# Attention with the values as the loaded operand and the output scaled by reciprocals spread from memory

## The reference

```python
q = (xn @ Wq).reshape(b, n, HEADS, DIM_HEAD).transpose(0, 2, 1, 3)
k, v = (kv[..., :DIM_HEAD], kv[..., DIM_HEAD:])
q = l2norm(q) * q_scale
k = l2norm(k) * k_scale
sim = jnp.einsum('bhid,bjd->bhij', q, k) * SCALE + attn_bias     # causal and masked
attn = jax.nn.softmax(sim, axis=-1)
out = jnp.einsum('bhij,bjd->bhid', attn, v)
return ln(out.reshape(b, n, HEADS * DIM_HEAD) @ Wout, g_out)
```

## Time and profile before

| what | value |
|---|---|
| median of 3 runs | 2564.28 us |
| profiled execution, first to last instruction (span) | 2563.2 us |
| attention, from the first scores to the first delta projection | 55 to 1101 us |
| TensorE busy, share of the span | 93% |
| VectorE / ScalarE / GpSimd busy | 68% / 48% / 52% |

### The profile page before, as it was taken

The page is one execution under the profiler, slowest core; times in us unless marked ns, Lnnn a source line. Parts: engine busy times, 40 slices in busy tenths (PEclk is TensorE's granted clock), DMA queues, the critical chain, the costliest instruction groups (busy, mean ns, idle before and its releaser), DMA issues. The chain is left out here.

```text
span 2563.2 us, 56453 instructions
## 1 busy us (share of the span) xinstructions
PE 2394.0 (93%) x20705; PEld 1977.5 (77%) x20705; DVE 1753.9 (68%) x4121; ACT 1234.0 (48%) x3133; POOL 1333.1 (52%) x1464
## 2 busy tenths in 40 slices
PE   5999999999999999977999999988899999999998
PEld 3788888888888888845777777766677877778776
DVE  4576767677767676677888888337865755746764
ACT  3656666666666666554555555114333333332332
POOL 3676767676767676535666666215422322322332
PEclk8999999999999999988999999999999999999999
DMA  4000100000000000001122221216022112111211
GB/s 143 7 11 9 46 18 11 10 10 9 11 10 9 10 5 5 5 15 24 40 56 55 55 53 47 55 59 181 32 66 63 55 58 67 58 47 62 66 34 59
DMA packets 156689, 105.05 MB, mean 41 GB/s; under 512 B 85168, under 2 KB 134832, under 8 KB 156416
## 3 DMA queue, kind: packets, MB, share of 16 engines
q1 hardware_dynamic: 130928, 62.69, 9.0%
q10 hardware_dynamic: 25488, 38.73, 4.9%
HBM read 80.51 MB, written 20.88 MB: 40 GB/s over the span
## 5 line engine op out<-in xcount | busy, mean ns | idle before, releaser
L968 POOL TENSOR_TENSOR a_bm<-a_bias,a_mask_add 128x512 f32<-128x512 f32 (+3 forms) x512 | 438.4, 873 | 189.3 <-DVE a_nm L697 186.3
L1592 POOL TENSOR_TENSOR m_hid_part<-m_hid,m_hid_part 128x512 fp32r<-128x512 f32 x176 | 238.5, 1355 | 552.9 <-ACT m_hid_part L1501 547.6
L874 ACT ACTIVATE a_S<-a_S,a_nm 128x512 f32<-128x512 f32 (+3 forms) x512 | 289.3, 565 | 347.6 <-DVE a_nm L697 344.9
L697 DVE CUSTOM_DVE_ANT_0 a_S<-a_S,a_bm,a_nsn 128x512 f32<-128x512 f32 (+3 forms) x512 | 275.3, 545 | 142.1 <-PE a_S L455 137.4
L478 PE MATMUL a_O<-a_v,a_PT 128*128 128x64 f32 x2560 | 342.4, 265 | 0.0
L478 PEld LDWEIGHTS a_O<-a_v,a_PT 128*128 128x128 f32 x2560 | 328.4, 193 | 0.0
L1513 ACT ACTIVATE m_hid<-m_G 128x512 f32<-128x512 f32 x176 | 105.4, 599 | 390.9 <-PE m_G L1447 353.3
L455 PE MATMUL a_S<-a_kT,a_qT 128*128 128x384 f32 (+3 forms) x1024 | 284.0, 358 | 3.6 <-DVE a_nm L697 3.2
L1674 DVE TENSOR_TENSOR m_hid<-m_hid,m_U 128x512 f32<-128x512 f32 x176 | 121.0, 687 | 223.8 <-PE m_U L1447 190.3
L1464 PE MATMUL m_Y<-m_hid_part,m_down_high 128*128 128x512 f32 x704 | 256.5, 405 | 12.2 <-POOL m_hid_part L1592 11.4
L1447 PE MATMUL m_G<-m_in,m_gate_high 128*128 128x512 f32 x704 | 252.2, 399 | 0.9 <-POOL m_up_low L1586 0.9
(11 more groups left out here) (323 smaller groups left out, 5348.4 us busy)
## 6 DMA issues: line engine op xcount, KB each, us to landing
m_spread<-s_w ACTq DMA_DIRECT2D x64, 256.0 KB, 3.2
m_spread<-s_w ACTq DMA_DIRECT2D x128, 128.0 KB, 2.9
a_x<-in_x SPq DMA_DIRECT2D x32, 128.0 KB, 2.2
s_hT<-a_hT SPq DMA_DIRECT2D x32, 128.0 KB, 2.1
d_x<-in_x SPq DMA_DIRECT2D x8, 512.0 KB, 4.7
d_h<-s_hT SPq DMA_DIRECT2D x8, 512.0 KB, 5.2
s_xg<-d_xg SPq DMA_DIRECT2D x8, 512.0 KB, 3.1
d_x<-s_xg SPq DMA_DIRECT2D x8, 512.0 KB, 4.6
```

The source lines that it names most:

```text
L697: dve.tensor_tensor_reduce(S[:, n % S_SLOTS, 0:w], SB[n % 2][:, 0:w], bm[:, n % BM_SLOTS, 0:w], -1.0, nsn[:, tile % 2, h:h + 1], ALU.add, ...
L874: act.activation(S[:, n % S_SLOTS, 0:w], S[:, n % S_SLOTS, 0:w], ACT.Exp, scale=-1.0, bias=nm[:, tile % 2, h:h + 1], accum_out=den[:, tile ...
L968: pool.tensor_tensor(bm[:, n % BM_SLOTS, 0:w], bias[:, h, L - w:L], mask_add[b % 2][:, 0:w], ALU.add).then_inc(s["bm_ready"], 1)
L1592: pool.tensor_tensor(hid_part[1][:, q % H_SLOTS], hid[:, q % G_SLOTS], hid_part[0][:, q % H_SLOTS].bitcast(F32), ALU.subtract).then_inc(hi ...
```

## The change

PV is turned round: the values (128 x 64) are loaded, and the turned exponentials (128 x 128) are streamed. The result comes out with the head's features along the partitions, two heads above one another (partitions 0 to 63 and 64 to 127), which is the layout that the output projection wants. So PV is done for a pair of heads in every second step, and the oT step goes away. A fourth PT buffer is added. The output can't be scaled by a value per partition any more; the reciprocals (8 heads x 128 queries) are turned by TensorE (new step wT0 for the first eight heads, the pnT step for the others), written to memory and read back spread over 64 partitions each (256 KB for eight heads), and VectorE multiplies PSUM by them into oT (new steps scale0 and scale1). Steps move, and some fill another bank.

```diff
-    QK_LAG, PV_LAG, S_SLOTS, PT_SLOTS = 2, 4, 5, 3
+    QK_LAG, PV_LAG, S_SLOTS, PT_SLOTS = 2, 4, 5, 4
...
-                 "null": 10, "qs0": 8, "qs1": 9, "qT0": 12, "qT1": 12, "qT2": 13, "qT3": 14}
-        BACK = {"diff1": 0, "weigh1": 4, "oT": 6, "pnT": 7, "outp": 9, "hn": 11, "hT": 13}
+                 "null": 10, "qs0": 8, "qs1": 9, "qT0": 11, "qT1": 12, "qT2": 13, "qT3": 13}
+        BACK = {"diff1": 0, "scale0": 1, "weigh1": 1, "pnT": 3, "scale1": 8, "outp": 9, "ostat": 11, "hn": 12, "hT": 14}
...
-                    behind.setdefault(NH * t + 10, []).append(("diff0", t))
-                    behind.setdefault(NH * t + 13, []).append(("weigh0", t))
+                    behind.setdefault(NH * t + 8, []).append(("diff0", t))
+                    behind.setdefault(NH * t + 9, []).append(("weigh0", t))
+                    behind.setdefault(NH * t + 10, []).append(("wT0", t))
...
-        FILLS = {"xT": 0, "q0": 1, "q1": 0, "kv": 1, "qT0": 0, "qT1": 1, "qT2": 0, "qT3": 1, "kT": 0,
-                 "pnT": 1, "outp": 0, "hT": 1, "nullo": 0, "wide0": 0, "wide1": 1}
+        FILLS = {"xT": 0, "q0": 1, "q1": 0, "kv": 1, "qT0": 0, "qT1": 0, "qT2": 0, "qT3": 1, "kT": 0,
+                 "pnT": 0, "outp": 1, "hT": 1, "wT0": 0, "nullo": 0, "wide0": 0, "wide1": 1}
...
+                    elif name in ("wT0", "pnT"):
+                        i = int(name == "pnT")
+                        sp.wait_ge(s["pnrT_ready" if i else "weightT_ready"], t + 1)
+                        sp.dma_start(weight_rows[i], pnrT[LATE, :] if i else weightT[:]).then_inc(weight_out, 16)
+                        sp.wait_ge(weight_out, 16 * (2 * t + 1 + i))
...
+                        for e in range(2):
+                            sp.dma_start(weight[e * DH:(e + 1) * DH, i].rearrange("p (a n) -> p a n", n=P),
+                                         bass.AP(tensor=weight_rows.tensor, offset=(i * NH // 2 + e) * P,
+                                                 ap=[[0, DH], [2 * P, NH // 4], [1, P]])).then_inc(weight_in[i], 16)
...
+                            at = h % 8 // 2 * P
                             for j in range(tile % TT + 1):
-                                last = pe.matmul(OB[h // 8][:, (h % 8) * DH:(h % 8 + 1) * DH],
-                                                 PT[:, n % PT_SLOTS, j * P:(j + 1) * P], v[tile // TT % 2][:, j],
-                                                 start=j == 0, stop=j == tile % TT)
+                                for e in range(2):
+                                    last = pe.matmul(OB[h // 8][e * DH:(e + 1) * DH, at:at + P], v[tile // TT % 2][:, j],
+                                                     PT[:, (n - 1 + e) % PT_SLOTS, j * P:(j + 1) * P],
+                                                     start=j == 0, stop=j == tile % TT, skip_group_check=True)
...
+                def scale(t, i):
+
+                    dve.wait_ge(weight_in[i], 32 * (t + 1))
+                    dve.wait_ge(s["pv_done"], NH // 2 * t + 4 * (i + 1))
+                    if t > 0:
+                        dve.wait_ge(full[1], filling["outp", t - 1, 1])
+                    dve.tensor_tensor(oT[:, 4 * i:4 * i + 4].rearrange("p a n -> p (a n)"), OB[i][:, :], weight[:, i],
                                       ALU.mult).then_inc(s["o_scaled"], 1)
```

More of the change, by code:

```diff
@@ L315, in drained @@
                     "qT2": [(s["qT_act"], 2 * t + 2)], "qT3": [(s["qT_dve"], 2 * t + 2)],
-                    "kT": [(s["kT_read"], t + 1)], "oT": [((s["oT_act"], s["oT_dve"])[n], t + 1)],
+                    "kT": [(s["kT_read"], t + 1)],
+                    "wT0": [(s["weightT_ready"], t + 1)],
                     "pnT": [(s["pnrT_ready"], t + 1)], "outp": [(s["hn_ready"], t + 1)],
@@ L468, in _ @@
                         n = t - PV_LAG
-                        if 0 <= n < NH * NT:
-                            tile, h = divmod(n, NH)
+                        if 0 <= n < NH * NT and n % 2 == 1:
+                            tile, h = divmod(n - 1, NH)
+                            wait_evac(pe, n - 1)
                             wait_evac(pe, n)
@@ L562, in _ @@
                         pe.transpose(f[:, 0:P], kn[:].rearrange("p a d -> p (a d)"), ident[:]).then_inc(full[0], 1)
-                    elif name == "oT":
-                        pe.wait_ge(s["o_scaled"], 2 * t + 2)
-                        for n in range(2):
-                            f = fill("oT", t, n)
-                            for j in range(4):
-                                i = 4 * n + j
-                                last = pe.transpose(f[:, j * P:(j + 1) * P],
-                                                    o[:, 2 * i:2 * i + 2].rearrange("p a d -> p (a d)"), ident[:])
-                            last.then_inc(full[n], 1)
+                    elif name == "wT0":
+                        pe.wait_ge(s["rden_ready"], 2 * t + 1)
+                        f = fill(name, t)
+                        pe.transpose(f[0:NH // 2, 0:P], rden[:, 0], ident[:]).then_inc(full[0], 1)
                     elif name == "pnT":
@@ L582, in _ @@
                             pe.matmul(f[:, 0:D], oT[:, i], wout[:, i], start=i == 0, stop=False)
-                        pe.matmul(f[:, 0:D], pnrT[:], null_out[:], start=False, stop=True).then_inc(full[0], 1)
+                        pe.matmul(f[:, 0:D], pnrT[:], null_out[:], start=False, stop=True).then_inc(full[1], 1)
                     elif name == "hT":
@@ L607, in weigh @@
                     link(dve.tensor_tensor(dent[:, i], den[:, c, hs], pn[:, i], ALU.add))
-                    link(dve.reciprocal(rden[:, i], dent[:, i]))
                     if t > 0:
-                        dve.wait_ge(full[1], filling["pnT", t - 1, 1])
-                    dve.tensor_tensor(pnr[:, hs], pn[:, i], rden[:, i], ALU.mult).then_inc(s["weights_ready"], 1)
-                    dve.wait_ge(s["pv_done"], NH * t + 8 * (i + 1))
+                        dve.wait_ge(full[0], filling[("wT0", "pnT")[i], t - 1, 0])
+                    to = pnr[:, LATE] if i else rden[:, 0]
+                    dve.reciprocal(to, dent[:, i]).then_inc(s["rden_ready"], 1)
+                    dve.wait_ge(s["rden_ready"], n)
                     if t > 0:
-                        dve.wait_ge(full[i], filling["oT", t - 1, i])
-                    dve.tensor_tensor(o[:, hs], OB[i][:, :].rearrange("p (h d) -> p h d", d=DH),
-                                      rden[:, i].unsqueeze(2).broadcast_to([P, 8, DH]),
+                        dve.wait_ge(full[0], filling["pnT", t - 1, 0])
+                    dve.tensor_tensor(pnr[:, hs], pn[:, i], to, ALU.mult).then_inc(s["weights_ready"], 1)
+                def scale(t, i):
[4 more added lines that the diff above has]
+                    dve.tensor_tensor(oT[:, 4 * i:4 * i + 4].rearrange("p a n -> p (a n)"), OB[i][:, :], weight[:, i],
                                       ALU.mult).then_inc(s["o_scaled"], 1)
@@ L768, in _ @@
                         weigh(t, int(name[5]))
-                    elif name == "oT":
-                        f = filled("oT", t, 1)
-                        if t > 0:
-                            dve.wait_ge(full[0], filling["outp", t - 1, 0])
-                        dve.tensor_copy(oT[:, 4:8].rearrange("p a n -> p (a n)"), f[:, :]).then_inc(s["oT_dve"], 1)
+                    elif name == "wT0":
+                        f = filled(name, t)
+                        dve.tensor_copy(weightT[:], f[0:NH // 2, 0:P]).then_inc(s["weightT_ready"], 1)
+                    elif name in ("scale0", "scale1"):
+                        scale(t, int(name[5]))
                     elif name == "pnT":
@@ L776, in _ @@
                         if t > 0:
-                            dve.wait_ge(full[0], filling["outp", t - 1, 0])
+                            dve.wait_ge(full[1], filling["outp", t - 1, 1])
                         dve.tensor_copy(pnrT[:], f[:, 0:P]).then_inc(s["pnrT_ready"], 1)
-                    elif name == "outp":
+                    elif name == "ostat":
                         f = filled("outp", t)
@@ L929, in _ @@
                         act.activation(pn[:, i], dn[:, i], ACT.Exp).then_inc(s["null_probs"], 1)
-                    elif name == "oT":
-                        f = filled("oT", t, 0)
-                        if t > 0:
-                            act.wait_ge(full[0], filling["outp", t - 1, 0])
-                        act.copy(oT[:, 0:4].rearrange("p a n -> p (a n)"), f[:, :]).then_inc(s["oT_act"], 1)
                     elif name == "hT":
```

34 lines of the change are left out of this document (22 added, 12 removed).

## The result

The changed kernel takes 2624.67 us (median of 4 runs, 2619.1 to 2630.4), the kernel before 2564.86 us beside it (4 runs, 2559.71 to 2566.23): a ratio of 1.0245, interval 1.0223 to 1.0267, or 60 us more. The forecast was 2585 us, with 2573 to 2612 as its own case and 2515 to 2628 as the wide range. The direction was right. The time lies just inside the wide range and outside the forecast's own case, and the loss is almost three times the one forecast (60 us against 21).

The account below looks back on a forecast made before the run. TensorE was taken to bound W4 outright, with a chain on other engines late next in W1. 2563 + 2 (windows) + 4 (end) + 16 (clock) = 2585 us; own case 2573 to 2612, 8 in 10 from 2515 to 2628.

Parts of the forecast that it names:

- PV's prices at all four widths: TensorE's time per pair of heads: 0.455, 0.675, 0.895 and 1.115 us in W1 to W4, 42 us less in all.
- VectorE held by pnT ahead of ss: Step 3: VectorE must wait for pnT's turn and copy it before ss, which starts at 8.35, 6.75, 8.05 and 9.4 us.
- TensorE before the key and before scale1: TensorE waits before kT 3.6, 3.1, 2.0, 0.9 us, and before outp a new 2.2, 1.9, 1.55, 1.05, W1 to W4.
- the spread hidden in the windows and bare at the end: The DMA pair through memory is in time in every window; behind the last head nothing hides it, +4 us.
- The waits that end with the key: TensorE's wait for the normed key at kT: 60 to 80 us in all, about 1 us before the change.
- the change doesn't do what it says: Rival: PV's accumulating matmuls don't run side by side in the array's halves; +86 us on PV, about 2650 us, chance 0.03.
- The clock did not stay: Denies the rival that the waits are there but TensorE's clock doesn't fall: 2569 us, chance 0.16.
- The work comes off: Rival: the waits are shorter, so TensorE's saved work shortens the kernel: 2504 us, or 2534 with half eaten; chance 0.28.
- More falls: Rival: the clock falls in W3 too and stays low through outp and query turns, 24 times 2.5 us: 2629 us, chance 0.08.
- the term for the windows, "+0.3 x 8, about +2 us": W1 to W4 laid out by hand: 29.8, 29.2, 32.8, 35.8 us, together 127.6 against 127.3, times eight sequences.
- the paragraph "Banks": Late steps of each window: statistics gain 0.5 to 1 us in W1, W2; qT1 waits 0.7 to 1.3, hT and xT up to 0.8.
- the clock's term: Clock falls in every W1 and half of the W2 windows, 12 at 1.3 us: +16 us.

Follow-up runs that it names:

- the better one: The changed kernel with kT at step 9 and the turns of the queries and output steps put back as before the change: 2539.5 us, ratio 0.9916.

## Why the prediction was too small

**Right.** PV's prices at all four widths; about 66 us less work on TensorE in 27 windows (the steps' prices give some 53); VectorE held by pnT ahead of ss; TensorE before the key and before scale1; the spread hidden in the windows and bare at the end (6.7 us by the run without it, 4 forecast); low clock most in W1, little in W2, none in W3. Up to the turn of the key the laying out by hand was good to a tenth of a microsecond: with the turns as before, ss starts at 8.34, 6.76, 8.13 and 9.41 us (8.35, 6.75, 8.05 and 9.4 forecast) and the key is turned at 13.82, 12.51, 14.16 and 15.71 (13.85, 12.5, 14.1 and 15.7).

**Smaller than its sign.** The waits that end with the key are 27.4 us in the whole run, where 60 to 80 were forecast; a part of the same delay stands under other names in steps 4 to 7 (1.13 and 0.33 us in the W1 shown). Those for scale1 are 39.4, with 5.9 of the end in them, for 50. And W4 was to get 2 to 3 us shorter; it went from 38.69 to 38.58.

**The rivals.** The new PV records are 0.055 us apart, so "the change doesn't do what it says" is out. The clock did not stay. "The work comes off" did not happen: with the turns as before, the waits, the low clock and the end together just take it up (2564.03 us). "More falls" has almost the measured time, 2629 us, and that is luck in the main: it wanted 24 falls at 2.5 us, W3 among them, and there are 18 stretches in the 27 windows, none in W3, which add 32.5 us and not 60.

**Wrong: the term for the windows, "+0.3 x 8, about +2 us".** At full clock they are longer than laid out. Taking the clock's share off the means, the four windows are 131.5 us together (33.87 + 30.18 + 33.62 + 38.58, less 3.59, 0.42 and 0.73), not 127.6: 3.9 us a sequence, 31 us in all. Two places make it up. The chain from ss to kT starts 0.4 to 0.8 us later than laid out in each window (means 9.11, 7.37, 8.79 and 9.79 us, against 8.35, 6.75, 8.05 and 9.4), 2.5 us over the four at kT. And behind kT W4's tail is 1.7 us longer than laid out at full clock, where qT1 waits for qT0's copy; the tails of the other three fit to 0.3 us.

The step that failed is the paragraph "Banks". It gave qT1 a wait of 0.7 to 1.3 us, hT and xT up to 0.8, took 0.5 to 1 us off for the statistics, and so had at most 1.6 us a window against the new order. Undoing the order brought 60.6 us, 1.9 a window, and putting it alone on the kernel before cost 43. Three things were wrong in it. qT1's wait reaches 1.95 us in W4, since it looked at ScalarE's own queue and not at what ScalarE's exponential waits for, VectorE's null operations in step 10. The late hT was priced at its turn and not in ScalarE's queue, where it stands ahead of the next tile's xnT and has a part in the late start of the next window's chain. And the statistics at step 11 were counted as a gain; moved to 10 they are worth nothing with qT1 in bank 0 and, with it in bank 1, are what that bank needs (34 us for the two edits). The forecast never asked what the old order would have given, and so did not see that the order alone stood between a loss and no change.

**Wrong: the size of the clock's term.** It was 12 falls at 1.3 us, 16 us. In the 27 windows the low level added about 32.5 us, 3.6 in each W1, 0.4 in W2 and 0.7 in W4. The 20 stretches are more than the 12 forecast; most lie in W1 (12 of the 18 in the 27 windows, 89 of 113 us), where they were forecast, and four at the end of W4, where none was. The price of one in W1 was taken from the earlier trace rows, where the projection lost 1.7 us. In the middle of W1 the low level covers the whole projection, which loses 2.6 us, and the steps around it lose another 1. The run with unread matmuls confirms a part of it (11 us of the median), and the edits that took waits away took low clock away too (122 us, then 95, 78, 65 and 37 in the runs with ss ahead, the turns as before, kT at 9, and all three; 78 also in the run with the turns and kT at 9 together, so it isn't in step with the time). So the price of a wait in this kernel is not the wait alone.

By stretches, in the two profiled executions: from the first window to the start of the last 64.1 us more (2 + 16 forecast); the last window and the end 1.1 us less, with the spread's 6.7 in them (4 more forecast); the first scores 2.3 us later; and behind the attention 7.3 us less, which the change doesn't touch. I have no cause for the last two, but they are no larger than the scatter: in the experiments' profiles the same two stretches take 54.5 to 57.8 and 1454 to 1467 us. Together 58 us, the spans' difference.

**Not settled.** The order isn't the only cure: kT at 9 leaves it as it is and brings 53 of the 60 us. How the 27 us of qT3 and hT split between the two was not tried, nor was qT0 at its old step 12. What an edit is worth depends on the others: ss ahead gave 28 us in the changed kernel and 19 in the better one, kT at 9 gave 53 and 25. They share waits, so the single gains don't add up.

## What to carry to other kernels

When a change replaces an operation and also reorders steps, price the reordering on the kernel before by itself: here it cost 43 us there, and it was the whole difference between no change and a loss. For steps that share a bank, follow the copy that frees it back through two engines, up to the longest instruction that it stands behind, and see which bank comes free first; a late copy costs nothing where the next step wants the other bank. Look also at what a later step now stands ahead of in the next round, as hT did ahead of xnT. And put the step that waits longest (here the turn of the key) as late as its reader allows, behind the engine's own work: where the clock falls in a wait, the work behind it is slower too (some 32.5 us in the 27 windows here).

## What I had not expected of the hardware

A fall of the granted clock lasts beyond the wait: in W1 it stood at 0.51 for the 5.5 us behind the wait with TensorE busy all the time, and 16 records of the projection took 6.32 us instead of 3.67. And VectorE's smallest two-input operations can be as long as the GpSimd operation beside them: in W4 L783 ends at 591.51 and GpSimd's operation beside it at 591.49, L784 at 592.74 beside 592.72. In all, L783 (128 x 16) takes between 0.15 and 1.25 us with a median of 0.45; in the W4 shown the time is GpSimd's, and it stood in the path of ScalarE's copy of qT0. The Trainium skill has a rule for it ("SBUF — State Buffer", SBUF: two separate sides): the port pair that the two engines share is a lock, and whichever of the two starts first holds it for the whole instruction. The two pairs of ends above agree. In W1 L783 ends at 492.69 beside a bias of 0.73 us that ends at 492.67, and L784 behind it, with GpSimd idle, takes 0.18 us.
